# Expert gate and up products with the weights held in TensorE and the tile's rows streamed

## The reference

```python
g = flat @ shared_gate.T
u = flat @ shared_up.T
shared_out = jax.nn.sigmoid(g) * u @ shared_down.T
weights = jax.nn.softmax(flat @ router_w.T, axis=-1)
top_w, top_idx = jax.lax.top_k(weights, 2)
...
ge = jnp.einsum('nh,eih->nei', xb, wg)      # bfloat16
ue = jnp.einsum('nh,eih->nei', xb, wu)
he = jax.nn.sigmoid(ge) * ue
de = jnp.einsum('nei,ehi->neh', he, wd)
routed = (comb[:, :, None] * de).sum(axis=1)
return x + shared_out + routed
```

## Time and profile before

| what | value |
|---|---|
| median of three runs | 331.34 us |
| the profiled execution, its span | 332.47 us, 330.7 us |
| TensorE, matmuls in flight (share of span) | 295.4 us (89%) |
| TensorE, weight loads | 208.7 us (63%) |
| VectorE, ScalarE, GpSimd | 216.4, 132.0, 158.8 us |
| tile stage, first to last gate/up product | 211.5 to 300.9 us |

### The profile page before, as it was taken

One profiled execution on the slowest core, in us unless ns is written; L12 is line 12 of the kernel. 1 busy time (PEld: TensorE's weight loads), 2 busy tenths in 40 slices (PEclk: granted clock), 3 DMA queues, 4 the chain that ended last, 5 costly groups with the idle time before them and its releaser, 6 DMA issues.

```text
span 330.7 us, 6138 instructions
## 1 busy us (share of the span) xinstructions
PE 295.4 (89%) x1596; PEld 208.7 (63%) x1608; DVE 216.4 (65%) x585; ACT 132.0 (40%) x235; POOL 158.8 (48%) x238
## 2 busy tenths in 40 slices
PE   7579789999999999999999998799999999997280
PEld 2247658786878776877887786566666666663120
DVE  0788878478756588745467488576777676775291
ACT  2263577606657406678104370134343434342000
POOL 3706892685701757402767046035565555565100
PEclk9999989999999999999999999999999999999587
DMA  7999699022060120000159994333434334339499
GB/s 247 342 229 319 98 210 291 27 96 79 20 237 0 50 80 0 0 4 0 64 116 210 208 207 154 83 89 121 124 100 110 113 97 126 98 99 314 134 316 343
DMA packets 30612, 45.91 MB, mean 139 GB/s; under 512 B 3008, under 2 KB 20160, under 8 KB 30592
## 3 DMA queue, kind: packets, MB, share of 16 engines
q1 hardware_dynamic: 20016, 27.66, 27.5%
q0 software_dynamic: 10432, 17.99, 22.9%
q10 hardware_dynamic: 144, 0.00, 0.0%
HBM read 39.58 MB, written 14.72 MB: 164 GB/s over the span
## 4 chain that ended last, share of the span: by engine, by line
PE 68%; DMA 7%; DVE 7%; POOL 7%; issue 6%; ACT 2%; SPq 1%; POOLq 0%; DVEq 0%; ACTq 0%
PE bank L677 13%; PE bank L472 11%; PE bank L473 11%; PE bank L474 11%; PE bank L694 7%; POOL xg L398 5%; PE bank L484 4%; PE bank L467 4%; PE bank L669 3%; PE bank L685 2%; DMA z<-ysb,desti 2%; DMA zb<-z 2%; DMA wqk_sb<-wqk 1%; DVE acc L1272 1%; DVE prob L951 1%
## 5 line engine op out<-in xcount | busy, mean ns | idle before, releaser
L888 ACT ACTIVATE sigc<-bank 128x352 f32<-128x352 f32 x39 | 18.1, 463 | 67.0 <-PE bank L677 67.0
L451 POOL DMA_INDIRECT z<-ysb,desti x36 | 36.1, 1002 | 9.6 <-issue 9.3
L472 PE MATMUL bank<-lnT_hi,sgu_lo 128*128 128x512 f32 (+2 forms) x96 | 39.1, 407 | 1.6 <-DVE lnT_lo L988 1.6
L473 PE MATMUL bank<-lnT_lo,sgu_hi 128*128 128x512 f32 (+2 forms) x96 | 37.8, 394 | 0.0
L474 PE MATMUL bank<-lnT_hi,sgu_hi 128*128 128x512 f32 (+2 forms) x96 | 37.8, 394 | 0.0
L398 POOL DMA_INDIRECT xg<-lnb,slot x32 | 31.9, 996 | 9.9 <-issue 7.6
L1239 DVE TENSOR_TENSOR hrow<-sigc,bank 128x352 bf16<-128x352 f32 x39 | 20.3, 521 | 24.3 <-ACT sigc L888 16.9
L677 PE MATMUL bank<-wgu_lo,xTb 128*128 x156 | 36.0, 313 | 0.0
L677 PE MATMUL bank<-wgu_hi,xTb 128*128 x156 | 36.0, 312 | 0.0
L387 POOL TENSOR_TENSOR hT_lo<-sig,hT_hi 128x512 fp32r<-128x512 f32 (+1 forms) x9 | 11.6, 1289 | 45.7 <-ACT hT_hi L800 45.7
L1245 DVE TENSOR_SCALAR ysb<-bank,wt 128x512 bf16<-128x512 f32 x39 | 29.1, 747 | 5.7 <-DMA z<-ysb,desti 2.8
(11 more groups left out here) (178 smaller groups left out, 651.1 us busy)
## 6 DMA issues: line engine op xcount, KB each, us to landing
xt<-xg SPq DMA_DIRECT2D x39, 129.0 KB
xT_raw<-xT SPq DMA_DIRECT2D x4, 1024.0 KB, 7.3
acc<-x SPq DMA_DIRECT2D x4, 1024.0 KB, 9.5
out<-acc SPq DMA_DIRECT2D x16, 256.0 KB, 3.5
wgu_lo<-wguT POOLq DMA_DIRECT2D x2, 1408.0 KB, 13.3
wgu_hi<-wguT POOLq DMA_DIRECT2D x2, 1408.0 KB, 13.3
cx<-ctxT SPq DMA_DIRECT2D x4, 512.0 KB, 4.3
wd_sb<-wdT POOLq DMA_DIRECT2D x2, 1024.0 KB
```

Of the source, the lines that this page charges most:

```text
L451: nc.gpsimd.indirect_dma_start(out=z, out_offset=bass.IndirectOffsetOnAxis(ap=desti[:, r:r + 1], axis=0), in_=ysb[:, r, :], in_offset=None ...
L472: pe.matmul(dst, a_lo, b_hi, start=first, stop=False)
L473: pe.matmul(dst, a_hi, b_lo, start=False, stop=False)
L888: act.activation(sigc[:, v, :], bank[2 * v][:, 0:I], ACT.Sigmoid).then_inc(s["csig"], 1)
```

## The change

Gate and up are computed transposed. The weights of the expert are the held operand, in three parts of 128, 128 and 96 columns (`KI`) for each half and each of the four parts of the contraction, and the 128 rows of the tile are streamed. The products land in PSUM as (hidden index, row), which is the form in which `narrow` needs them; `turn_hidden`, ScalarE's copy `hidden_out`, and the buffer `hrow` are gone, and VectorE writes `hTb` itself. `narrow` runs one step earlier (for tile u - 2).

```diff
-                    for k in range(NT):
-                        mm = pe.matmul(bank[2 * v + half_][:, 0:I], xTb[:, v, k, :], wgu(k, bass.ds(e, 1), half_ * I, I),
-                                       start=(k == 0), stop=(k == NT - 1))
+                    for c in range(IT):
+                        for k in range(NT):
+                            mm = pe.matmul(bank[2 * v + half_][0:KI[c], c * P:(c + 1) * P], wgu(k, bass.ds(e, 1), half_ * I + c * P, KI[c]),
+                                           xTb[:, v, k, :], start=(k == 0), stop=(k == NT - 1))
                 mm.then_inc(s["cgu"], 1)
-
-            def turn_hidden(u, v):
-                pe.wait_ge(s["ch"], u + 1)
-                at_least(pe, s["cev"], u)
-                for k in range(IT):
-                    mm = pe.transpose(bankHT[:, k * P:(k + 1) * P], hrow[:, v, k * P:(k + 1) * P], identb[:])
-                mm.then_inc(s["ct"], 1)
 
             def narrow(u, v, e):
-                pe.wait_ge(s["cev"], u + 1)
+                pe.wait_ge(s["ch"], u + 1)
                 at_least(pe, s["yev"], u - 1)
...
                 if not known or 2 <= u <= NE + 1:
-                    turn_hidden(u - 2, r % 2)
-                if not known or u >= 3:
-                    narrow(u - 3, (r - 3) % 2, ids[r])
+                    narrow(u - 2, r % 2, ids[r + 1])
...
-                act.activation(sigc[:, v, :], bank[2 * v][:, 0:I], ACT.Sigmoid).then_inc(s["csig"], 1)
-
-            def hidden_out(u, v):
-                act.wait_ge(s["ct"], u + 1)
-                at_least(act, s["cy"], u - 1)
-                act.copy(hTb[:, v], bankHT[:, 0:IT * P].rearrange("p (k l) -> p k l", k=IT)).then_inc(s["cev"], 1)
+                act.activation(sigc[:, v, :], bank[2 * v][:, 0:IT * P], ACT.Sigmoid).then_inc(s["csig"], 1)
...
-                at_least(dve, s["ct"], u - 1)
-                V.tensor_tensor(hrow[:, v, 0:I], sigc[:, v, :], bank[2 * v + 1][:, 0:I], ALU.mult).then_inc(s["ch"], 1)
+                at_least(dve, s["cy"], u - 1)
+                V.tensor_tensor(hTb[:, v], sigc[:, v, :].rearrange("p (k l) -> p k l", k=IT),
+                                bank[2 * v + 1][:, 0:IT * P].rearrange("p (k l) -> p k l", k=IT), ALU.mult).then_inc(s["ch"], 1)
...
-                if not known or 3 <= u:
-                    result(u - 3, (r - 3) % 2, (r - 3) % SLOTS, q if r == 3 else q - 1)
+                if not known or 2 <= u:
+                    result(u - 2, r % 2, (r - 2) % SLOTS, q if r >= 2 else q - 1)
```

More of the change, by code:

```diff
@@ L78, in gated_block @@
         bankXT = bank[4][:, :].bitcast(BF16)
-        bankHT = bank[5][:, :].bitcast(BF16)
         small_sb = sb("small_sb", [P, 4])
@@ L178, in gated_block @@
         (sd_raw,), _ = place((("sd_raw", [P, IT, N], F32),), lnT_end)
-        (xt, xTb, hrow, hTb, sigc, ysb), c_end = place((
-            ("xt", [P, SLOTS, ROW], U32), ("xTb", [P, 2, NT, P], BF16), ("hrow", [P, 2, IT * P], BF16),
-            ("hTb", [P, 2, IT, P], BF16), ("sigc", [P, 2, I], F32), ("ysb", [P, SLOTS, N], BF16)), top)
+        (xt, xTb, hTb, sigc, ysb), c_end = place((
+            ("xt", [P, SLOTS, ROW], U32), ("xTb", [P, 2, NT, P], BF16), ("hTb", [P, 2, IT, P], BF16),
+            ("sigc", [P, 2, IT * P], F32), ("ysb", [P, SLOTS, N], BF16)), top)
         assert c_end <= lnT_end
@@ L206, in gated_block @@
             "xmm x1 base lgcopy lgT lgshift rexp pick order weight rank place placed scat rowsb rowsb2 sgate sup sigd hid hhi hlo dm shared "
-            "sent packed xT_in padrows padout tabs cxt xev cgu csig ch ct cev cy yev dchain pchain hot didx za_in zsum comb outd").split()}
+            "sent packed xT_in padrows padout tabs cxt xev cgu csig ch cy yev dchain pchain hot didx za_in zsum comb outd").split()}
         s_xl = [sem(f"xt_in{i}") for i in range(SLOTS)]
@@ L724, in _ @@
                     step(q, r, ids)
-            for u in range(SLOTS * QN, NE + 3):
+            for u in range(SLOTS * QN, NE + 2):
                 if u % SLOTS == 0:
@@ L899, in step @@
                     sigmoid(u - 1, (r - 1) % 2)
-                if not known or 2 <= u <= NE + 1:
-                    hidden_out(u - 2, r % 2)
             for r in range(SLOTS):
@@ L907, in _ @@
                     step(q, r)
-            for u in range(SLOTS * QN, NE + 2):
+            for u in range(SLOTS * QN, NE + 1):
                 step(u // SLOTS, u % SLOTS)
@@ L1218, in _ @@
             hidden_low_last(2)
-            link(V.memset(hrow[:, :, I:IT * P], 0.0))
             tables_rows()
```

## The result

The changed kernel takes 400.07 us, the median of four runs (399.14 to 400.73), against 331.3 us before: ratio 1.206, 95% interval 1.202 to 1.210. The profiled execution took 400.73 us with a span of 399.0 us. The forecast was 398 us, range 388 to 412. In the experiments some executions ran in a slower state, 1 to 2% longer at a slightly lower granted clock: ratios and intervals leave these out, the medians of times don't.

A forecast was written before the change was run, and what follows sets the result against it. TensorE's sequencer, not its array, was taken to bound the kernel. Address operations 73.6 us, less 4.7 for the removed transposes and 2.4 at the stage's end, give 66.5 us on the median of 331.34: 398 us, range 388 to 412.

The forecast's parts named there:

- The bound and the mechanism: Gate and up, TensorE's sequencer: one register operation per product, 16 more a tile at 0.118 us, none hidden, 73.6 us.
- The tile stage: Tile stage: 73.6 us of added address operations less 4.7 us for the removed transposes; 155 to 160 us long.
- The end of the stage: From last product to first `zb` read: 8.84 us before, 6.4 us expected with late stores free, 2.4 us saved.
- It has nothing to spare: Kernel before, tile loop: the iteration's 9.50 us are TensorE's sequencer's sum, 3 x 2.1 and 3.2 with the head.
- 1 (addresses shared): Gate and up: column parts share one address operation or the offset is free; array bounds, 324 us; chance 0.06.
- 2 (slow pairs): Gate and up: addresses cheap but load-and-matmul pairs slow at 0.109 us, 373 us; chance 0.08.
- 3 (a load at a register address not overlapped): Gate and up: such a pair takes 0.153 us, 16 us above the forecast, 414 us; chance 0.06.
- 4 (code fetched again): Tile loop: TensorE's longer code is fetched again each pass, 15 us more, 412 us; chance 0.08.
- The signs: Profile after: 936 register operations, issue spread over all tiles, 16.5 us an iteration, TensorE in flight much less than 97%.
- The clock: Tile stage: a clock fallen throughout makes a tile 4.3 us against 4.14 of issue, at most 6 us more.

The follow-up runs named there:

- experiment 1: The kernel before with each gate and up product split in three, 24 matmuls at 24 register addresses a tile, rows still held: 406.21 us, ratio 1.222.
- experiment 2: The changed kernel with the gate half reading expert 0's weights at a fixed address, the up half keeping its register: 347.87 us in one execution.
- experiment 7: The kernel before with VectorE copying the next tile's rows to xTb before it scales the finished result: ratio 0.998 (0.993 to 1.003).
- experiment 6: The kernel before without two waits of the gate and up step that earlier waits of the same queue already cover: ratio 0.999 (0.996 to 1.003).
- experiment 3: The changed kernel with gate and up both at expert 0's fixed address, no register addresses at that line: 331.73 us, ratio 0.993.
- experiment 10: The changed kernel with six more 512-column products on fixed operands at the end of each loop iteration: 402.09 us, ratio 1.209.
- experiment 5: The kernel before with each gate and up product split in three, all at expert 0's fixed address: 332.68 us in one execution.
- experiment 9: The changed kernel without the two covered waits of the gate and up step: 397.5 us, ratio 1.198 (1.191 to 1.206).

## Why the prediction was right, and where it was not

*The bound and the mechanism* held. Each product at a register address costs the sequencer one operation, none is shared, and the 16 added a tile aren't hidden. An operation was priced at 0.118 us; 0.119 (experiment 1) and 0.123 (experiment 2, which also loses part of the slow table read) were measured.

*The tile stage* grew from 89.35 to 160.6 us, by 71.2. The steps gave 73.6 - 4.7 = 68.9. The missing 2.3 us are mostly a term that the sum didn't have: the read of the experts' word takes 0.6 instead of 0.3 us in six of the loop's seven iterations, 1.9 us in all. Without it an iteration would be about 16.6 us, and the prediction had 16.5. It isn't the length of the loop body, since experiment 1 has a longer one and its reads have the old length:

```profile
L662 PEldq TENSOR_LOAD <-epack_i x11: 298/303/490, 211.8 to 376.7; - x11
```

The cause is open.

*The end of the stage*: 6.4 us were worked out for the way from the last product to the first `zb` read. The last product ends at 371.36 and the read is issued at 377.21:

```profile
370.99 0.37 PE L677 MATMUL bank<-xTb,wgu_hi 128*96 128x128 bf16 x2
...
372.71 0.35 PEld L687 LDWEIGHTS bank<-wd_sb,hTb 128*128 128x128 bf16 x3 [1.02 <-issue]
...
374.69 0.97 POOL L442 DMA_INDIRECT z<-ysb,dest  x1 [0.30 <-DVE ysb L1229]
377.21 0.81 SPq L291 DMA_DIRECT2D zb<-z  x2
```

5.85 us: 3.0 saved instead of 2.4, the late stores gone as predicted.

*"It has nothing to spare"*, said of the sequencer in the kernel before, was too strong. It was right for the loop's head and wrong within the tiles, where it also waited for VectorE's copy. The step added up the starts of sequencer instructions and took all time between them for work; a part, about 0.17 us an iteration by experiment 7, was a wait. For this change that didn't matter, because an added operation lies on the path either way. It mattered for the improvement in experiment 6, which failed by it.

*The rivals.* 1 (addresses shared) and 2 (slow pairs) fell with the counts and with experiment 3: pairs of 128 columns ran at 0.056 us, not 0.109. The Trainium skill ("TensorE: Matmul & The Clock Gate", "Back-to-back issue gap") gives 81 ns for such a pair; the measurement decides. 3 (a load at a register address not overlapped) fell: 24 pairs took 2.57 to 2.76 us, 0.11 us each and not 0.153. 4 (code fetched again) fell too: 13 fetches instead of 10 fit the longer program read once, since seven passes that fetched again would need at least seven more, and the branch still takes 218 to 242 ns. By the section "ISA Cache" of the Trainium skill's "Advanced Engine Details and Errata" it should be so, and the trace agrees.

*The signs* that the prediction named were worse than its sum. The count of operations (936), the iteration, the stage (160.6 us for 155 to 160) and the end (5.85 us for 6 to 7) came out or nearly so. But "issue" didn't spread over the tiles of the chain, and TensorE wasn't in flight much less: 147.06 of the stage's 160.60 us, and 11.04 of 11.10 in the row above. And one gap of over 1 us in each iteration, the sign of rival 4, did stand in the trace without that rival: the head of 1.79 us. The kernel before has that head too, but there most of it was covered by products already handed over (its chain has 0.26 us of issue there).

*The clock* did fall, once in an iteration; the prediction allowed up to 6 us for it, experiment 10 found none. At 1.2 GHz 128 columns take 0.107 us (the 24 products in 2.57 us from 260.60 on), still less than the sequencer's step. `narrow` and the transposes fall behind there, with 0.98 and 0.43 us for 0.82 and 0.23, and the products behind them make it up.

## What to carry to other kernels

Count the products that read at a run-time address, not only the columns they stream: the sequencer pays about 0.12 us for each, so by an estimate from this kernel a product has to stream some 280 columns at the full clock before its address is free (352 columns take 0.149 us, so 0.118 us are 279). A transposed form that saves work on the array can lose to that count; multiply it out before changing the shape.

When a sequencer is the bound, look for its waits too. An edit that frees time ahead of a wait that another engine ends late gains little until that engine's order is changed as well, so try the two together before either is given up.

## What the runs showed that was not expected

- The read of the experts' word into a register on TensorE took a median of 0.55 us in the changed kernel and 0.51 in experiment 10, and was slow in some iterations of experiments 5 and 9; in the loops of the kernel before and of the other experiments it was 0.3 to 0.4. Nothing tried here explains it.
- A matmul group whose loads are of 96 columns (listed at 119 to 123 ns, against 98) kept the pace of the 128-column ones: 24 pairs in 1.34 us.
- With fixed addresses TensorE's sequencer was 14 to 17 products ahead at the loop's end, whether these lasted 1.7 us or 0.7 us: short products shorten its lead in time, and the loop's head shows.
- TensorE, idle for 1.8 us at the loop's head and half occupied elsewhere, ran at 1.2 GHz for 3.4 us behind that gap, at no cost to the kernel; six products in the gap kept it at 2.4 GHz.
